# Residual sums through identity products in PSUM at two layer boundaries, and the second attention head's weights in two transfers

## What is computed

```python
x = x + L0_gnn(layernorm(x), ...)      # two graph attention layers: 8 heads of 768, then 1 head
x = x + L0_ffn(layernorm(x), ...)      # 8 experts, best two, plus a spectral term
x = x + L1_gnn(layernorm(x), ...)      # one graph convolution
...
def gat_layer(x, W, a_s, a_d, b, edges):
    h = (x @ W).reshape(n, H, C)
    e = leaky_relu(alpha_s[src] + alpha_d[dst])     # alpha = h . a, per head
    alpha = segment_softmax(e, dst)
    return segment_sum(h[src] * alpha, dst) + b
```

## Time and profile before

| | us |
|---|---|
| median of three runs (351.64 to 352.48) | 352.17 |
| the profiled execution | 351.26 |
| its span, first to last instruction | 349.4 |
| PE busy in it (share) | 339.2 (97%) |
| DVE, ACT, POOL busy | 178.2, 67.8, 38.8 |

### The profile page before, as it was taken

The page is one execution under the profiler, slowest core; times in us unless marked ns, Lnnn a source line. Parts: engine busy times, 40 slices in busy tenths (PEclk is TensorE's granted clock), DMA queues, the critical chain, the costliest instruction groups (busy, mean ns, idle before and its releaser), DMA issues.

```text
span 349.4 us, 4172 instructions
## 1 busy us (share of the span) xinstructions
PE 339.2 (97%) x1581; PEld 215.3 (62%) x1585; DVE 178.2 (51%) x534; ACT 67.8 (19%) x157; POOL 38.8 (11%) x64
## 2 busy tenths in 40 slices
PE   7999999999999999989999999999999999999997
PEld 3565656565656666546555655576646698966754
DVE  4946345666747485566773753542852501172431
ACT  2002011010101111102110331014314412073120
POOL 4900000020000000232022000021230100000000
PEclk9999999999999999999999999999999999999999
DMA  8999999999882858998999667576725800000001
GB/s 285 428 374 429 430 411 419 425 423 364 319 317 91 325 218 336 427 387 307 395 428 385 258 252 267 176 276 237 270 64 234 305 12 0 2 0 3 0 0 45
DMA packets 10501, 90.18 MB, mean 258 GB/s; under 512 B 2169, under 2 KB 2822, under 8 KB 6386
## 3 DMA queue, kind: packets, MB, share of 16 engines
q1 hardware_dynamic: 8238, 84.91, 61.5%
q0 software_dynamic: 848, 3.61, 3.0%
q10 hardware_dynamic: 1396, 1.40, 1.2%
HBM read 89.53 MB, written 0.39 MB: 257 GB/s over the span
## 4 chain that ended last, share of the span: by engine, by line
PE 87%; DVE 6%; DMA 3%; issue 1%; SPq 1%; ACT 0%; POOL 0%; DVEq 0%
PE ps L1562 16%; PE ps L1528 15%; PE ps L1507 7%; PE ps L1951 7%; PE ps L1754 5%; PE ps L1735 4%; DMA ring<-in_gat_w 3%; PE ps L1550 3%; PE ps L1628 2%; PE ps L2063 2%; PE ps L2022 2%; PE ps L2083 2%; PE ps L1868 2%; PE ps L1984 1%; PE ps L1650 1%; PE ps L1439 1%
## 5 line engine op out<-in xcount | busy, mean ns | idle before, releaser
L1528 PE MATMUL ps<-ring,xT 128*128 128x512 f32 (+1 forms) x168 | 56.7, 486 | 0.5 <-DMA ring<-in_gat_w 0.5
L1562 PE MATMUL ps<-ring,h 128*128 128x512 f32 (+1 forms) x168 | 55.6, 486 | 0.0
L1562 PEld LDWEIGHTS ps<-ring,h 128*128 128x128 f32 x168 | 31.2, 190 | 21.9 <-issue 20.1
L1528 PEld LDWEIGHTS ps<-ring,xT 128*128 128x128 f32 x168 | 30.9, 191 | 19.6 <-issue 16.6
L812 DVE CUSTOM_DVE_ANT_0 g<-h,avec 128x768 f32<-128x768 f32 x8 | 7.7, 958 | 35.3 <-ACT h L518 21.8
L518 ACT ACTIVATE h<-ps 128x768 f32<-128x768 f32 (+6 forms) x24 | 13.8, 576 | 60.2 <-PE ps L1528 16.2
L1507 PE MATMUL ps<-ring,xT 128*128 128x512 f32 (+1 forms) x72 | 24.1, 488 | 0.1
L904 DVE TENSOR_SCALAR ring<-ring,idxb,ewb 128x128 bf16<-128x128 bf16 x99 | 22.5, 305 | 0.0
L1507 PEld LDWEIGHTS ps<-ring,xT 128*128 128x128 f32 x72 | 13.4, 190 | 9.3 <-issue 8.4
L402 POOL TENSOR_TENSOR rstd<-var,mhalf 128x1 f32<-128x1 f32 x8 | 4.7, 583 | 118.1 <-DVE var L1392 53.4
L1754 PE MATMUL ps<-ring,h 128*128 128x512 f32 (+1 forms) x48 | 16.4, 492 | 0.0
(11 more groups left out here) (413 smaller groups left out, 484.7 us busy)
## 6 DMA issues: line engine op xcount, KB each, us to landing
ring<-in_gat_w SPq DMA_DIRECT2D x15, 2304.0 KB, 11.9
avec<-in_gat_a SPq DMA_DIRECT2D x9, 768.0 KB, 10.0
ring<-in_l_w SPq DMA_DIRECT2D x3, 2304.0 KB, 18.5
ring<-in_gat_w SPq DMA_DIRECT2D x6, 384.0 KB, 5.7
ring<-in_l_w SPq DMA_DIRECT2D x2, 1152.0 KB, 12.5
ring<-in_l1f_w1a SPq DMA_DIRECT2D x1, 2304.0 KB, 12.5
ring<-in_l1f_w1b SPq DMA_DIRECT2D x1, 2304.0 KB, 10.8
ring<-in_l1f_w2a SPq DMA_DIRECT2D x1, 2304.0 KB, 14.6
```

The source lines that it names most:

```text
L1528: last = mm(ps[:, at + lo:at + hi], xT[:, c, :], w[:, c, lo:hi], start=(c == 0), stop=(c == C - 1))
L1562: last = mm(ps[:, 4 * WIN + lo:4 * WIN + hi], h2[:, par * D + c * P:par * D + (c + 1) * P], w[:, c, lo:hi], start=(n == 0 and c == 0), sto ...
```

## The change

Three edits. (1) The weights of head 1 come in two transfers of half the columns' chunks each; the vector of head 0 stands between them. Head 1's product waits for the first, and for the second only before its fourth chunk. The score row of head 0 moves one chunk further back, and the turn of its attention from between the column parts to the middle of the second part. Two warm-up products at the start are dropped. (2) At the first boundary PE multiplies `xb` with the identity into the banks ahead of the attention product, which then adds onto it; DVE measures the sum where it lies in PSUM (`measure`), ACT copies it to x, and the centring waits for the copies. Four of the edge sums go from ahead of the product to behind it, and seven warm-up products are dropped. (3) At the second boundary the same with x itself: its two identity products take the place of two groups of warm-up products among the green levels.

```diff
@@ SP @@
-            load_w1(1, 1)
+            half = UNIT // 2
+            w1_1 = a["gat_w1"][1:2].rearrange("o p n -> (o p) n")
+            sp.dma_start(ring[:, 1, 0:half], w1_1[:, 0:half]).then_inc(S["w1_second_in"], 16)
             load_avec(0)
+            sp.dma_start(ring[:, 1, half:UNIT], w1_1[:, half:UNIT]).then_inc(S["w1_in1"], 16)
@@ ACT @@
+            def residual_rows(k, at):
+                for n, (lo, hi) in enumerate(HALVES):
+                    act.wait_ge(s("measured"), 2 * k - 1 + n)
+                    copy(x[:, lo:hi], ps[:, at + lo:at + hi]).then_inc(s(("x_part", "residual")[n]), 1)
+            residual_rows(1, 0)
             part_T(2)
...
             copy(wuT, bank(6, C * (DOWN + 1))).then_inc(s("l2_copied"), 1)
+            residual_rows(2, WIN)
             act.wait_ge(s("l2_ps"), 2)
@@ DVE: centre, and normalise in the same way @@
-            def centre(k):
+            def centre(k, copied=None):
...
+                    if copied is not None:
+                        dve.wait_ge(s(("x_part", "residual")[n]), copied)
                     nc.vector.tensor_scalar(xn[:, lo:hi], x[:, lo:hi], mv[:, 0:1], None, ALU.subtract) \
@@ DVE @@
-            dve.wait_ge(S["xb_ready"], 1)
-            add_residual(1, 0, xb)
-            centre(2)
+            def measure(k, at):
+                for n, (lo, hi) in enumerate(HALVES):
+                    dve.wait_ge(s("rows_ps"), 2 * k - 1 + n)
+                    nc.vector.bn_stats(stats[:, n, :], ps[:, at + lo:at + hi]).then_inc(s("measured"), 1)
+                dve.wait_ge(s("measured"), 2 * k)
+            measure(1, 0)
+            centre(2, copied=1)
...
-            add_residual(2, WIN, x)
-            normalise(3, xn, x, "xn_ready")
+            measure(2, WIN)
+            normalise(3, xn, x, "xn_ready", copied=2)
@@ PE: head_product @@
-                pe.wait_ge(S[f"w1_in{par}"], in_value)
+                if n == 1:
+                    pe.wait_ge(S["w1_second_in"], 16)
+                else:
+                    pe.wait_ge(S[f"w1_in{par}"], in_value)
...
+                        if n == 1 and c == 3 and lo == parts[0][0]:
+                            pe.wait_ge(S["w1_in1"], in_value)
+                        if n == 1 and c == 4 and lo == parts[0][0]:
+                            score_row(0, 0)
+                        if n == 1 and c == 3 and lo == parts[1][0]:
+                            turn_attention(0)
@@ PE @@
-            stay_warm(12)
+            stay_warm(10)
...
-                score_row(0, 0)
-            head_product(1, 1, 16, lambda: turn_attention(0), count_edges).then_inc(S["hprod"], 1)
+            head_product(1, 1, 16, halfway=count_edges).then_inc(S["hprod"], 1)
...
             score_row(8, 0)
-            sum_edges(range(14, 29))
+            pe.wait_ge(S["xb_ready"], 1)
+            for lo, hi in HALVES:
+                mm(ps[:, lo:hi], ident, xb[:, lo:hi], start=True, stop=False)
+            sum_edges(range(14, 25))
             turn_attention(8)
...
-                mm(ps[:, lo:hi], attnT[:, 0, :], h1[:, lo:hi], start=True, stop=True).then_inc(s("rows_ps"), 1)
-            sum_edges(range(29, EC)).then_inc(s("edges_summed"), 1)
-            warm_until(9, "var_ready", 2)
+                mm(ps[:, lo:hi], attnT[:, 0, :], h1[:, lo:hi], start=False, stop=True).then_inc(s("rows_ps"), 1)
+            sum_edges(range(25, EC)).then_inc(s("edges_summed"), 1)
+            warm_until(2, "var_ready", 2)
             stay_warm(1)
...
             shift_green(3)
-            stay_warm(4, 1)
+            pe.wait_ge(s("residual"), 1)
+            mm(ps[:, WIN:2 * WIN], ident, x[:, 0:WIN], start=True, stop=False)
             shift_green(4)
...
-            stay_warm(2, 1)
+            mm(ps[:, 2 * WIN:WIN + D], ident, x[:, WIN:D], start=True, stop=False)
             shift_green(5)
...
                     last = mm(ps[:, WIN + lo:WIN + hi], h1[:, H0 + c * P:H0 + (c + 1) * P], w[:, c, lo:hi],
-                              start=(c == 0), stop=False)
+                              start=False, stop=False)
```

More of the change, by code:

```diff
@@ L208, in s @@
             return S[name]
-        for name in ("x_in w1_first0_in w1_first1_in w1_first2_in w1_first3_in w1_first4_in cols_in graph_in small_in avec_in w1_in0 w1_in1 w2_in0 w2_in1 w2_used hprod "
+        for name in ("x_in w1_second_in w1_first0_in w1_first1_in w1_first2_in w1_first3_in w1_first4_in cols_in graph_in small_in avec_in w1_in0 w1_in1 w2_in0 w2_in1 w2_used hprod "
                      "h_rows alpha_ready score_sum negmax exped "
@@ L755, in whiten, with normalise @@
                 dve.wait_ge(s("rstd_ready"), k)
-            def normalise(k, dst, src, signal):
+            def normalise(k, dst, src, signal, copied=None):
                 whiten(k)
-                for lo, hi in ((0, D // 2), (D // 2, D)):
+                for n, (lo, hi) in enumerate(((0, D // 2), (D // 2, D))):
+                    if copied is not None:
+                        dve.wait_ge(s(("x_part", "residual")[n]), copied)
                     nc.vector.tensor_scalar(dst[:, lo:hi], src[:, lo:hi], mv[:, 0:1], rstd[:], ALU.subtract, ALU.mult) \
                         .then_inc(s(signal), 1)
-            def centre(k):
+            def centre(k, copied=None):
                 link(nc.vector.bn_aggr(mv[:], stats[:].rearrange("p a b -> p (a b)")))
                 nc.vector.tensor_scalar(var[:], mv[:, 1:2], LN_EPS, None, ALU.add).then_inc(s("var_ready"), 1)
-                for lo, hi in ((0, D // 2), (D // 2, D)):
+                for n, (lo, hi) in enumerate(((0, D // 2), (D // 2, D))):
+                    if copied is not None:
+                        dve.wait_ge(s(("x_part", "residual")[n]), copied)
                     nc.vector.tensor_scalar(xn[:, lo:hi], x[:, lo:hi], mv[:, 0:1], None, ALU.subtract) \
```

## The result

Over 21 runs of each kernel the median went from 351.76 us (351.28 to 352.76) to 350.01 us (348.83 to 352.61): ratio 0.9947, 95% interval 0.9937 to 0.9958, a gain of 1.75 us where 0.95 was forecast. The time lies inside the stated range of 349.8 to 352.3 by 0.2 us, outside the forecast's own range of 350.8 to 351.6, and nearer to rival (a)'s 349.8 than to the 351.2 of the sum. The median before is 0.41 lower over 21 runs than over the three that the prediction had. The slowest run of the new kernel, 352.61, shows a mean granted clock of 0.995 where the others show 0.999 or 1.00; without it its runs spread over 2.8 us.

The account below looks back on a forecast made before the run. TensorE bounds the kernel (87% of the span), so savings count only where PE waits. First edit 0, first boundary 0.85, second 0.1: 0.95 us off the 352.17 median gives 351.2 us; own range 350.8 to 351.6, stated range 349.8 to 352.3.

Parts of the forecast that it names:

- rival (a): Start: the 1.4 us lead lives, vectors of heads 1 and 3 land over a microsecond earlier; 349.8 us, chance 0.14.
- First edit: Head 1's split weights, moved score row and turn: PE's 1.4 us lead is lost to later vectors; booked 0.
- PE waits about 1 us: Sign that the forecast is right: PE waits this long at head 2's score transpose or turn.
- Nothing in this chain is issued by PE late enough to matter; it hangs on the stream: Start to head 3's turn: the DMA stream sets the time, so the lead of 1.4 us is booked as 0.
- a saving is taken off the median unchanged: Whole kernel: savings worked out on the profiled 351.26 us are subtracted from the median of 352.17.
- that work starts when a transfer lands: Heads 1 and 3: DVE's work on the attention vectors starts at a landing and ends just as PE wants it.
- First boundary: Two adds of about 1.1 us leave DVE's chain; PE sets the transposes' new start, 0.85 us gained.
- Second boundary: DVE loses about 1.1 us of adds, but PE waited only 0.23 us there; 0.1 us gained.
- The green levels: Two identity products on x replace warm-up products of the same length; 0, at most 0.1 us.
- (b): Boundaries give almost nothing: copies and statistics serialise, or identity products overrun the 0.81 us idle; 352.0 us, chance 0.19.
- (c): Start loses its clock with fewer warm-up products, head 0's product ends 1.5 us later; 352.7 us, chance 0.09 including slower stream.

Follow-up runs that it names:

- after_again: The new kernel, unchanged, profiled once more: 349.90 us.
- e5: The new kernel with two buffers for the attention vectors, each vector issued one head earlier: median 348.51 us, ratio 0.9893 to the old kernel.
- before_again: The old kernel, unchanged, profiled a second time: 352.20 us.
- e2: The old kernel with only the two boundaries changed, the start as before: median 350.68 us, ratio 0.9965 to the old kernel.
- before_third: The old kernel, unchanged, profiled a third time: 351.93 us.
- e3: The new kernel with twelve warm-up products at the start again in place of ten: median 350.44 us, ratio 0.9954 to the old kernel.
- e4: The new kernel without the three warm-up products at either boundary: median 349.19 us, ratio 0.9917 to the old kernel.
- e1: The old kernel with only the first edit, two warm-up products fewer included: median 351.31 us against 352.04, ratio 0.9978.
- e7: The old kernel with only head 1's weights split into two transfers, nothing moved: median 351.75 us, ratio 0.998 to the old kernel.

## Why the prediction was right, and where its size was off

The direction, and every place that it named, came out; the time lies at the low edge of the stated range, and that it lies inside is in part luck, as the range reached down for rival (a), whose sign no profile of after shows. 351.2 less 350.01 is 1.2 us, in three pieces: 0.41 is the median before, which was 352.17 over three runs and 351.76 over 21; 0.34 is the boundaries with what stands behind them, 1.29 us (below) where 0.95 was booked; the 0.45 that is left is the first edit, booked at 0.

**First edit, booked at 0.** Right in its mechanism: no wait at the first chunk, none for head 0's attention, a lead that z of head 0 takes back ("PE waits about 1 us": 0.97, and 0.54 in after_again), head 3's vector on its old time (55.42 against 55.4 foretold), its turn at 67.69 against 67.8. e5 shows the lead of 1.4 to be real and the vectors to be what held it. The step that failed is the 0 itself, by way of two sentences: "Nothing in this chain is issued by PE late enough to matter; it hangs on the stream", which holds for the profiled execution and not for an ordinary one (in before_again and e2 head 3's attention is ready 1.1 to 1.2 us before PE comes, in before_third 0.3), and "a saving is taken off the median unchanged". 0 was the difference to an execution in which PE had waited only 0.46 us for the weights and so met the vector with nothing to spare. A tie to a transfer is a tie to a point in time, not a saving: in after, PE stands at the turn at 67.44 to 67.87 (after, after_again, e3, e4), whatever it did before. In an ordinary run of before PE gets there at 68.3 to 68.4. The edit is worth the difference: 0.77 between the means of the two ordinary profiles of before and of the two of after, 0.77 by the ratio of e1 (0.73 by its medians) and 0.70 by that of e7 (0.37 by its medians), both with wide intervals, and 0.45 as what the boundaries leave of the 1.75. So its size is known to about 0.4 to 0.8 us. The 0.91 us between the profile and the median stood in the prediction, and its place in the trace was not asked for; it was in large part this wait. One reading of the rows was wrong without harm: "that work starts when a transfer lands" is true of head 3, but in the earlier trace rows head 1's alphas start on ScalarE's copy (27.68), 0.2 us after the transfer; the sum used the transfer's 27.5.

**First boundary, 0.85 forecast.** 0.91 measured (4.25 to 3.34), in the profiles of after, after_again and e2 alike. The terms: the identity products took the 0.81 us of idle time down to 0.17 and did not overrun it; statistics read from PSUM cost 1.03 for both halves where 0.69 and 0.4 were taken; ScalarE's copies took 0.87 and ran in part beside them; PE was the last, which e4 confirms.

**Second boundary, 0.1 forecast.** 0.15 measured. That three warm-up products hid more is shown by e4: without them 0.66 us.

**The green levels** and the stretch behind the second boundary, booked at 0, gave 0.08 and 0.15: from the transposes to the combine product 17.48 where the two ordinary profiles of before have 17.56, and from the aggregation to the end of the execution 169.5 where they have 169.66. With the two boundaries that is 1.29 us, and e2, which has nothing else, gave 1.23 by its ratio and 1.36 by its medians. The whole sum, ordinary profiles against those of after, is 0.77 + 0.91 + 0.08 + 0.15 + 0.15 = 2.06, where the executions differ by 2.05; the medians say 1.75, since these two of before lie 0.3 above the median of the 21; that leaves 0.45 and not 0.77 for the first edit.

**Rivals.** (a) gave 349.8, and the time is near it, but not by its mechanism: its sign was to be a turn of head 3 near 66.5 with earlier vectors, and neither profiled execution of after shows one (67.69, 67.44). It takes e5 to make it so. What happened in the fastest runs of after, which go down to 348.83, no profile shows; there the lead may have lived in part. (b) fell: nothing serialised. (c) the prediction would have read from a product of head 0 ending after 15.6, and it ended at 7.82 + 7.95 = 15.77. That sign was a poor one: in after_again it ended at 15.42, and e3 shows a later start still that costs nothing. The terms of (c) were off as well: it let ten warm-up products end at 5.7, with the rise of the rate after the seventh, and they took 4.45 us from 2.10 on, all ten at 0.43. The Trainium skill (DMA: Bandwidth & Descriptors, section Anatomy of one DMA) would, if its fixed part of about 2.0 us were paid in the stream, have had head 3's vector land later by that much, as an estimate, with one transfer more. Its alphas began on it at 55.42, 55.17, 55.46, 55.61 and 55.68 in five executions with the split (after, after_again, e3, e4, e7), against 55.53 and 55.73 without (before, before_third); in before_again and e2, without it, the vector was there by 55.00 and 55.10. So 2.0 us are not paid there in any of these, though some tenths may be; the one execution with the split that was 2 us late (e1, 57.32) was the slowest of its kernel. The page's figure is for transfers issued by GpSimd; these are SyncE's.

## What to carry to other kernels

Where a gain ends in a wait for a transfer, work out the point in time at which that transfer lands and compare it with where an ordinary run stands, not with the one profiled; if the profiled execution lies outside the other runs, find in its trace what was early before any sum is made against it. A wait that is taken away in front of a buffer with one copy is half a change: the other half is the second buffer, and neither shows its full worth alone. And where PE fills a gap with products nobody reads, bringing forward what the gap waited for gives little until those products go too (0.15 us at the second boundary, and 0.66 more when they went).

## What the runs showed of the hardware

The first microseconds of the stream differ between executions, of the same program by up to 10% (352 and 387 GB/s from 2.5 to 9 us in two executions of after; 344 to 387 over all thirteen profiles), and then settle (427 to 435 from 9 to 16 us). And the rise of TensorE's rate does not come at the same product each time: the ten warm-up products of after took 4.45 us, 0.43 each and the way through the array, the rate of 1.2 GHz, and in its first profile the six transposes behind them still took 1.38 us, where those of after_again took 0.94. Where twelve such products stand there, they took from 4.08 us (before_again) to 5.30 (e3). The granted clock reads 1.00 throughout in all of these.
